# Cross attention in a Perceiver-like fp32 program: keys and values computed ahead in other stages and kept in DRAM

## The reference

```python
x = x + xattn0(norm(x), ctx)            # causal; attn16 in the kernel
x = x + rwkv(norm(x))
x = x + moe_pairs(norm(x))              # 24 experts, top 2
x = x + xattn(norm(x), ctx, mask)       # x1: mask * -1e9 added to the scores
x = x + attn8(norm(x))
x = x + butterfly_ffn(norm(x))
x = x + xattn(norm(x), ctx, log(w))     # x2: log weights of the keys added
x = x + rglru(norm(x))
x = x + moe_capacity(norm(x))           # 8 experts and a fallback, top 2
x = x + xattn(norm(x), ctx, seq == 0)   # x3: scores of such keys replaced
...
def xattn(q_in, ctx, extra):            # 16 heads of 8
    q, k, v = q_in @ Wq + bq, ctx @ Wk + bk, ctx @ Wv + bv
    p = softmax(q k^T / sqrt(8) + extra)
    return (p v) @ Wo + bo
```

## Time and profile before

| | us |
|---|---|
| median of 3 runs (lowest, highest) | 3881.17 (3876.15, 3885.0) |
| the profiled execution, its own time | 3872.74 |
| its span in the trace | 3870.9 |

### The profile page before, as it was taken

The page is one execution under the profiler, slowest core; times in us unless marked ns, Lnnn a source line. Parts: engine busy times, 40 slices in busy tenths (PEclk is TensorE's granted clock), DMA queues, the critical chain, the costliest instruction groups (busy, mean ns, idle before and its releaser), DMA issues. The chain is left out here.

```text
span 3870.9 us, 103050 instructions
## 1 busy us (share of the span) xinstructions
PE 2843.8 (73%) x27576; PEld 2254.0 (58%) x27577; DVE 2626.9 (68%) x9070; ACT 1653.2 (43%) x5099; POOL 1510.8 (39%) x1417
## 2 busy tenths in 40 slices
PE   5872478569999788527999992158849999967662
PEld 3652377447777677414777771057727777746552
DVE  5977522378888655674888885862158888869635
ACT  1112034247777422213777775303317777721111
POOL 1520067425655300140655550006615555525252
PEclk9985599879999899758999996558969999979765
DMA  2000244411111000200232220104533444400122
GB/s 79 0 0 21 83 130 146 125 34 35 36 35 36 17 1 0 103 0 22 72 69 70 70 54 0 31 22 139 134 84 104 105 103 104 95 1 0 33 78 72
DMA packets 212939, 226.48 MB, mean 59 GB/s; under 512 B 30981, under 2 KB 180485, under 8 KB 212167
## 3 DMA queue, kind: packets, MB, share of 16 engines
q1 hardware_dynamic: 200166, 199.36, 19.1%
q0 software_dynamic: 12672, 25.98, 2.5%
HBM read 202.69 MB, written 22.55 MB: 58 GB/s over the span
## 5 line engine op out<-in xcount | busy, mean ns | idle before, releaser
L1656 POOL TENSOR_TENSOR sx<-sx,rs 128x1028 f32<-128x1028 f32 x384 | 731.6, 1905 | 590.3 <-DVE rs L1787 590.3
L1735 ACT ACTIVATE sx<-sx,nm 128x257 f32<-128x257 f32 x1536 | 770.8, 505 | 349.1 <-DVE nm L1781 349.1
L1781 DVE CUSTOM_DVE_ANT_0 sx<-bank,rows 128x257 f32<-128x257 f32 x1024 | 394.1, 422 | 77.3 <-PE bank L1725 72.2
L1408 ACT ACTIVATE hT<-bank,B 128x128 f32<-128x128 f32 x714 | 205.5, 367 | 324.0 <-PE bank L1376 323.9
L1735 ACT ACTIVATION_READ_ACCUMULATOR sx<-sx,nm 128x1 f32 x1536 | 290.6, 189 | 0.0
L1725 PE MATMUL bank<-kT,qb 32*128 32x257 f32 x3072 | 276.1, 429 | 3.5 <-DVE nm L1781 3.4
L1797 DVE COPY pt<-bank 128x512 f32<-128x512 f32 x384 | 263.5, 686 | 4.6 <-PE bank L1676 4.6
L1676 PE MATMUL bank<-C,sx 128*128 128x128 f32 x1536 | 251.9, 287 | 3.7 <-DVE a L1830 3.4
L1434 DVE TENSOR_TENSOR yb<-bank,b2s 128x128 f32<-128x128 f32 x159 | 46.4, 292 | 304.7 <-PE bank L1389 303.2
L1691 PEld LDWEIGHTS bank<-W,ct 128*128 128x128 f32 x1536 | 235.0, 194 | 21.5 <-DVE vs L1809 0.5
L1688 PE MATMUL bank<-ct,W 128*128 128x257 f32 x768 | 235.0, 388 | 17.0 <-DVEq L1768 15.5
(11 more groups left out here) (383 smaller groups left out, 6260.3 us busy)
## 6 DMA issues: line engine op xcount, KB each, us to landing
ct<-in_ctxT SPq DMA_DIRECT2D x384, 128.5 KB
W<-in_L_w SPq DMA_DIRECT2D x159, 256.0 KB
rows<-rows_x SPq DMA_DIRECT2D x256, 128.5 KB
keep<-rows_keep SPq DMA_DIRECT2D x128, 128.5 KB
yg<-copy_outs SPq DMA_DIRECT2D x40, 256.0 KB
token_rows<-XN SPq DMA_DIRECT2D x24, 256.0 KB, 2.3
vl<-last_v SPq DMA_DIRECT2D x384, 2.0 KB
W<-in_L_w SPq DMA_DIRECT2D x39, 128.0 KB
```

The costliest lines, as they stand in the source:

```text
L1656: pool.tensor_tensor(sx[:, j, :, 0:KEYS], sx[:, j, :, 0:KEYS], rs[:, j, :].unsqueeze(2).to_broadcast([P, 4, KEYS]), ALU.mult).then_inc(p_r ...
L1735: ins = act.activation(sx[:, j, h, 0:KEYS], sx[:, j, h, 0:KEYS], ACT.Exp, bias=nm[:, j, h:h + 1], scale=-1.0, accum_out=sm[:, j, h:h + 1])
L1781: dve.tensor_tensor_reduce(sx[:, j, h, 0:KEYS], B[h][:, 0:KEYS], add, -1.0, 3.0e38, ALU.add, ALU.min, nm[:, j, h:h + 1]).then_inc(s_summed ...
```

## The change

A class `Ahead` numbers 384 jobs, one per batch of x1, x2 and x3. A job loads `ct_ahead` (128.5 KB; in x3 also `keep_ahead`, which GpSimd multiplies into `ctk`), computes the keys into B[6] and the values into B[7], copies both on ScalarE into `kv_out` (a ring of four), and stores them (256.5 KB) in DRAM as `kv_x1`, `kv_x2` or `kv_x3`. All jobs of a layer are done before its attention begins. They are shared out over other stages by `early` numbers: norms 6 (in moe 4), rwkv and rglru 5 per group of eight, "pairs" route, place and combine 16 each, `key_rows` 8, the butterfly's weight stage 75, "capacity" route 24, place 16, combine 12; what is left when the layer's own projection comes (16, 35 and 20) is done there. In these stages the jobs stand on TensorE ahead of, between or behind the stage's own instructions, as the diff shows, and likewise on ScalarE and SP. The loops of rwkv and rglru over groups are written out. The combining stage's `yg` has eight buffers in place of four.

In `xattn` the key and value matmuls and their copies are gone. SP loads `kv` (256.5 KB per batch, ring of eight), the scores read its keys and the value product its values. The value product goes into B[4], a bank of its own; the `pl` transpose into B[5]; the output product into a free part of B[0]. The copy of `pl` is on ScalarE (L1918) in place of VectorE. The reductions are four in a row, ahead of VectorE's `pt` copy. The pipeline drains one step later (DEPTH 8).

The diff, cut:

```diff
+        def ahead_moves(sp, count):
+
+            for n in ahead.next("sp", count):
+                name, b = ahead.job(n)
+                if n == 0:
+                    for first in range(3):
+                        ahead_load(sp, first)
+                ahead_load(sp, n + 3)
+                sp.wait_ge(*ahead.v_ready(n + 1))
+                sp.dma_start(T["kv_" + name][b], kv_out[:, n % 4, :]).then_inc(ahead.stored[n % 4].sem, 16)
+
+        def ahead_keep(pool, count):
+
+            for n in ahead.next("pool", count):
+                name, b = ahead.job(n)
+                if name == "x3":
+                    pool.wait_ge(*ahead.loaded[n % 4](ahead.loads_to(n)))
+                    pool.wait_ge(*ahead.k_psum(n - 1))
+                    pool.tensor_tensor(ctk[:, n % 2, :], ct_ahead[:, n % 4, :], keep_ahead[:, n % 4, :], ALU.mult)\
+                        .then_inc(ahead.kept.sem, 1)
+
+        def ahead_matmuls(pe, count):
+
+            for n in ahead.next("pe", count):
+                name, b = ahead.job(n)
+                pe.wait_ge(*ahead.loaded[n % 4](ahead.loads_to(n)))
+                if name == "x3":
+                    pe.wait_ge(*ahead.kept(b + 1))
+                pe.wait_ge(*ahead.k_ready(n))
+                pe.matmul(B[6][:, 0:KEYS], w(name + "_k"), ctk[:, n % 2, :] if name == "x3" else ct_ahead[:, n % 4, :],
+                          start=True, stop=True).then_inc(ahead.k_psum.sem, 1)
+                pe.wait_ge(*ahead.v_ready(n))
+                for c in range(2):
+                    ins = pe.matmul(B[7][:, c * P:(c + 1) * P], ct_ahead[:, n % 4, c * P:(c + 1) * P], w(name + "_v"),
+                                    start=True, stop=True)
+                ins.then_inc(ahead.v_psum.sem, 1)
+
+        def ahead_copies(act, count):
+
+            for n in ahead.next("act", count):
+                name, b = ahead.job(n)
+                act.wait_ge(*ahead.stored[n % 4](n // 4))
+                act.wait_ge(*ahead.k_psum(n + 1))
+                act.activation(kv_out[:, n % 4, 0:KEYS], B[6][:, 0:KEYS], ACT.Identity,
+                               bias=v(name + "_bk" if name != "x3" else "zero")).then_inc(ahead.k_ready.sem, 1)
+                act.wait_ge(*ahead.v_psum(n + 1))
+                act.copy(kv_out[:, n % 4, KEYS:KV], B[7][:, 0:2 * P]).then_inc(ahead.v_ready.sem, 1)
+
...
@@ norm
+                        ahead_moves(sp, early)
...
+                    ahead_copies(act, early)
                     act.wait_ge(*var_ready(1))
...
@@ rwkv
-                    with act.Fori(0, GROUPS) as g:
-                        rg = RT[:, bass.ds(g * GW, GW)]
+                    for g in range(GROUPS):
+                        rg = RT[:, g * GW:(g + 1) * GW]
                         act.activation(rg, rg, ACT.Sigmoid).then_inc(exp_ready.sem, 1)
+                        ahead_copies(act, early)
+
...
+                    for g in range(GROUPS):
+                        q = g % 2
+                        ahead_matmuls(pe, early)
+                        pe.wait_ge(*scan_ready(g + 1))
+                        pe.wait_ge(*x_added(g - 1))
...
@@ rglru
                             act.activation(a2[:, q], a2[:, q], ACT.Exp, scale=0.5).then_inc(y_done.sem, 1)
+                            ahead_copies(act, early)
...
+                        ins.then_inc(y_psum.sem, 1)
+                        ahead_matmuls(pe, early)
...
@@ route
                         act.activation(G[:], G[:], ACT.Exp).then_inc(b_done.sem, 1)
+                    ahead_copies(act, early)
...
+                    ahead_matmuls(pe, early)
+                    if kind == "capacity":
                         for e in range(E):
                             pe.wait_ge(*c_done(e + 1))
...
@@ sparse_experts, the combining stage
                     for gr in range(GROUPS):
-                        if gr >= RING:
-                            sp.wait_ge(*x_added(gr - RING + 1))
                         for k in range(K):
-                            sp.dma_start(yg[:, gr % RING, k], outs[:, k, gr * GT:(gr + 1) * GT, :]).then_inc(back[gr % RING].sem, 16)
+                            sp.dma_start(yg[:, gr, k], outs[:, k, gr * GT:(gr + 1) * GT, :]).then_inc(back[gr].sem, 16)
...
@@ xattn
-                project([(QT, w(name + "_q"), XNT, v(name + "_bq" if bias else "zero"), 8 ** -0.5)])
+                project([(QT, w(name + "_q"), XNT, v(name + "_bq" if bias else "zero"), 8 ** -0.5)],
+                        early=ahead.left(name))
...
+                    for j in range(4):
+                        sp.wait_ge(*ahead.stored[j](done // 4))
+                    for b in range(8):
+                        load(b, b)
+                        if b < 4:
+                            load_rows(b, b)
...
-                            pe.wait_ge(*a_ready(b - 1))
...
+                            pe.wait_ge(*pT2_ready(b))
...
-                        b, j = x, r_ % 4
-                        if ok(b):
-                            pe.wait_ge(*loads[j](per_load * (i * (U // 4) + r_ // 4 + 1)))
-                            pe.wait_ge(*k_ready(b))
-                            pe.matmul(B[4][:, 0:KEYS], w(name + "_k"), ct[j][:], start=True, stop=True).then_inc(k_psum.sem, 1)
-                            pe.wait_ge(*v_ready(b))
-                            for c in range(2):
-                                ins = pe.matmul(B[5][:, c * P:(c + 1) * P], ct[j][:, c * P:(c + 1) * P], w(name + "_v"),
-                                                start=True, stop=True)
-                            ins.then_inc(kv_psum.sem, 1)
...
+                            pe.wait_ge(*pl_ready(b))
+                            pe.transpose(B[5][:, 0:P], sx[:, j].rearrange("p h k -> p (h k)")[:, 32:1056:8], ident).then_inc(pl_psum.sem, 1)
...
-                            pe.matmul(B[6][:, 0:P], vl[:, j8, :], pl[:, q, :], start=True, stop=True)
+                            pe.matmul(B[4][:, 0:P], vl[:, j8, :], pl[:, q, :], start=True, stop=True)
+                            pe.wait_ge(*pT_ready(b + 1))
+                            pe.wait_ge(*pT2_ready(b + 1))
...
+                        if r_ % 4 == 2 and ok(x - 10):
+                            pe.wait_ge(*o_ready(x - 6))
+                            pe.wait_ge(*s_summed(4 * (x - 1 if ok(x - 1) else N)))
+                            pe.matmul(B[0][:, 3 * P:4 * P], oT[:, (r_ - 10) % 8 // 4, :], w(name + "_o"), start=True, stop=True)\
+                                .then_inc(y_psum.sem, 1)
...
-                                pe.matmul(B[h][:, 0:KEYS], qb[p, q].rearrange("p j s -> p (j s)"), kT[p, q, :],
+                                pe.matmul(B[h][:, 0:KEYS], qb[p, q].rearrange("p j s -> p (j s)"), kv[p, j8, 0:KEYS],
...
                             act.copy(pt[:, q, 1, :], B[7][:]).then_inc(pT2_ready.sem, 1)
+                            act.wait_ge(*pl_psum(b + 1))
+                            act.copy(pl[:, q, :], B[5][:, 0:P]).then_inc(pl_ready.sem, 1)
                         if ok(x - 2):
                             exps(x - 2, (1, 2, 3), (r_ - 2) % 4).then_inc(exp_done.sem, 1)
-                        b, q = x, r_ % 2
-                        if ok(b):
-                            if keep is None:
-                                act.wait_ge(*k_psum(b + 1))
-                                act.wait_ge(*scores(4 * (b - 1)))
-                                act.activation(kT[:, q, :], B[4][:, 0:KEYS], ACT.Identity, bias=v(name + "_bk")).then_inc(k_ready.sem, 1)
-                            else:
-                                act.wait_ge(*kv_psum(b + 1))
-                                act.wait_ge(*av_psum(b - 7))
-                                act.copy(vs[:, r_, :], B[5][:, 0:2 * P]).then_inc(v_ready.sem, 1)
...
-                            reduce(b, j, (0, 1))
+                            if rows is not None:
+                                dve.wait_ge(*rows_loaded[j](b // 4 + 1 if isinstance(b, int) else i * (U // 4) + (r_ - 2) // 4 + 1))
+                            reduce(b, j, (0, 1, 2, 3))
...
-                        if ok(x - 2):
-                            reduce(x - 2, (r_ - 2) % 4, (2, 3))
...
-                            dve.wait_ge(*pl_psum(b + 1))
-                            dve.wait_ge(*av_psum(b - 1))
-                            dve.tensor_copy(pl[:, q, :], B[7][:, 0:P]).then_inc(pl_ready.sem, 1)
...
@@ butterfly_ffn
+                    norm(fetch=fetch, early=early)
...
                         pe.matmul(B[2][:, 0:P], ones_row, r("down_bias"), start=False, stop=True)
+                        ahead_matmuls(pe, early_weights)
                         pe.wait_ge(*a_done(1))
...
@@ calls
+        norm(early=6)
+        moe("pairs", 24, 2, 4, 2 * TILES + 24 - 1, GW0[:], GB[:], T["L0_w1"], T["L0_b1"], T["L0_w2"], T["L0_b2"], True,
+            early=(4, 16, 16, 16))
+
+
+        key_rows(8)
+        norm(early=6)
+        attn8(6)
+        butterfly_ffn(6, 75)
+
+        norm(early=6)
```

(35 more changed lines are left out.)

280 lines of the change are left out of this document (158 added, 122 removed).

## The result

The changed kernel takes 4413.18 us (4405.31 to 4421.33) against 3880.73 before: 1.1375 times as long, 95% interval 1.1355 to 1.1394. The forecast was 4041, the range 3940 to 4130. The sign was right and the size was not: +533 us where +160 was forecast.

The account below looks back on a forecast made before the run. TensorE was taken to bound the attention before, a ring of VectorE and ScalarE after. Job costs 305 less gain 145 give +160: 4033 from the profiled 3872.7, which lies 8.4 under the median, so 4041 us, range 3940 to 4130.

Parts of the forecast that it names:

- The price of a job: Outside the attention, a job was to take 1.35 us in x1 and x2, and 1.85 in x3.
- in and out (385 KB) is 1.47: Outside the attention, a job's load and store were to take all DMA engines 1.47 us, at 0.49 per 128.5 KB.
- the store and reload collide: Rival: writing 98 MB makes each job 2.5 us; projects cost 178, routes, places, rglru 90 more; about 4200 us; chance 0.07.
- Where the groups land: Cost of the jobs in each host stage, such as projects 106, rglru 62, "capacity" routing 36; together 305 us.
- The ring: In the attention, VectorE and ScalarE waiting on each other set a batch's period, 3.43 us (bounds 3.26 and 3.52).
- The copy's 0.17: In the attention, the pl copy moved to ScalarE was to add 0.17 us to a batch's period.
- 0.19 from `rs` to the next reduction: In the attention, VectorE's step from rs to the next reduction was counted as 0.19 us of a batch's period.
- The twelve costs: What the jobs add in twelve groups of host stages, from 0 in rwkv to 106 in projects; summed to 305 us.
- The first rival: In the attention TensorE's 2.85 us sets the period: 358 us saved, jobs cost about 305, total 3828 us; chance 0.06.
- Ring does not bind: The first rival: in the attention TensorE's 2.85 us sets the period; 3828 us, chance 0.06.
- Jobs are hidden: Rival: ScalarE and TensorE idle in most host stages, so job costs halve; 3889 us; chance 0.08 over 3850 to 3950.
- The clock falls: Rival: in the attention the clock goes to 0.50 and TensorE's 2.85 us doubles to 5.7; about 4920 us; chance 0.03.

Follow-up runs that it names:

- e8: The changed kernel with the DRAM rows of the stored keys and values padded from 2052 to 2112 bytes: 4148.90 us, ratio to before 1.0693.
- e4: The changed kernel, rows unpadded, with the pl copy put back on VectorE behind its pt copy: ratio to before 1.131.
- e5: The changed kernel with padded DRAM rows and, in the attention, ScalarE's four Exps ahead of its pt and pl copies: 3902.45 us, ratio to before 1.0075.
- e7: As e5, but only x2 is computed ahead, with 128 jobs; x1 and x3 run the attention of before: 3780.47 us, ratio to before 0.9744.
- e10: The kernel before the change with one edit, ScalarE's four Exps ahead of its pt copy in the attention: 4647.38 us, ratio to before 1.1974.

## Why the prediction was wrong, step by step

- **The price of a job failed.** The step "in and out (385 KB) is 1.47" priced a store by the DMA time of a load. Loads it had right: 256.5 KB cost 0.92 us, and aligned stores 0.81. But a store of 2052-byte rows back to back cost 2.4 us in rwkv. With jobs 2.87 apart (3.06 over routing and placing), rwkv was not covered (+53), the routes grew by 43 and 47 instead of 21 and 36, the placing of "pairs" by 22 instead of 2, the butterfly by 98 instead of 24. Some 265 us are this one term (the ratios of the changed kernel and of e8). The rival "the store and reload collide" had the mechanism nearest to it, at 2.5 us a job, but it was set beside a row about loads, and its 4200 counted neither rwkv nor the butterfly.
- **Where the groups land was right.** With aligned rows the growth is: route of "pairs" 21.6 (forecast 21), its placing 2.7 (2), "capacity" route 39.5 (36), its placing 21.6 (19), rwkv with its norm 1.8 (1), butterfly 33.2 (24). Low were rglru, 76.9 with its norm (63), and the combining of "pairs" with key_rows, 26.6 (19): a group in rglru takes 21.7 where 20.5 was worked out. The norms grew by some 20 us together where 6 was forecast, and a job of x3 took 2.04 in the "capacity" route and the last projection where 1.85 was taken.
- **The ring was right, its size short.** The forecast period was 3.43, measured 3.54 and 3.62. The copy's 0.17 stands (e4: 0.14). The failing term is the "0.19 from `rs` to the next reduction", read in the head of x3; in the steady loop of the changed kernel it is 0.30 in x1,

```profile
1302.24 0.18 DVE L1951 RECIPROCAL rs<-sm 128x4 f32<-128x4 f32 x1 [0.60 <-ACT sx L1907]
1302.54 0.43 DVE L1945 CUSTOM_DVE_ANT_0 sx<-bank,maskq 128x257 f32<-128x257 f32 x1
```

and 0.38 in the median of x2 and x3, where the program adds a wait for `rows`. In the changed kernel's own head it is down to 0.20 and 0.26, so a head is not the loop. The steady loop of before could not have given the number either: there the two are 0.49 apart, with a wait for TensorE between them. At (3.54 − 3.43) × 127 + (3.62 − 3.43) × 254, 62 us of the gain went there. The rest, aligned, is 274 − 160 = 114: these 62 and some 50 of small misses among the hosts.
- **Slips in the sums.** The twelve costs add up to 307 and not 305, and the saving at a period of 3.52 is 102 and not 106; neither changes the argument. The first rival's 3828 takes the jobs at 305, which is the middle sum, and calls it their low bound; with the 240 that the prediction gives for the low bounds it would be 3763.
- **The rivals.** *Ring does not bind* is out (VectorE waits 0.60 for ScalarE), and e5 shows what it would have been worth: 2.93. *Jobs are hidden* is out for most hosts and true for those of e7. *The clock falls* is out: 1.00 in the attention with TensorE 116.45 of 150 us busy. The Trainium skill's statement that the full clock does not engage for transposes ("TensorE: Matmul & The Clock Gate", Part 4: PE-mode transpose) did not matter here: 378 of the 1504 matmuls whose records fall in this stretch are transposes, 50 of its 117 busy us, and the clock stayed at 1.00. That does not refute it, since the stretch is not of transposes alone. Nor did speak as clearly as the prediction has it: 9 of its 29 matmuls are transposes, 1.3 of 2.16 us.

## What to carry to other kernels

Price a store by a store, not by a load of its size: if the profile shows none like it, keep a multiple open in the range, and start every row that is written to DRAM on a multiple of 64 bytes. Work moved to "idle" engines is free only where it is off the path on each queue that it passes: count the hosts' free slots first, move that many, and leave the rest where it was (e7 moved a third of the jobs, with padded rows and the Exps first, and is the only version that gained). In a software pipeline, look for cycles over two steps as well as one: moving three Exps ahead of two copies on ScalarE's queue (e5) took 0.6 us off each batch, more than the change itself had gained there, and in the kernel before, without the separate banks, the same edit was a loss of 20% (e10).
